# Gated cross-attention and mixture block on one core: the value matmuls with float32 values as 32-column weights in four column groups and float32 probabilities moving

## The reference, cut to what matters

```python
# x (32, 128, 128), ctx_768 (32, 77, 96); H = 16 heads of hd = 8, E = 8 experts, 2 taken
xn, xfn = layer_norm(layer_norm(x)), layer_norm(ctx)
q = (xn @ Wq + bq).reshape(B, T, H, hd)
k = (xfn @ Wk + bk).reshape(B, N, H, hd)
v = (xfn @ Wv + bv).reshape(B, N, H, hd)
w = softmax(einsum('bthd,bnhd->bhtn', q, k) / sqrt(hd))
x = x + tanh(g_xattn) * einsum('bhtn,bnhd->bthd', w, v).reshape(B, T, D)
f = layer_norm(x)
top_vals, top_idx = top_k(f @ w_router, 2)
h = square(relu(einsum('nc,ecd->ned', f, w1)))
y = einsum('ned,edc->nec', h, w2)
x = x + tanh(g_ffn) * sum(take(y, top_idx) * softmax(top_vals))
```

## Time and profile before

| | |
|---|---|
| median of 3 runs | 432.58 us |
| the profiled execution | 432.84 us |
| its span (first to last instruction) | 431.0 us |
| granted TensorE clock, mean | 0.761 |
| PE busy | 72%, 2664 matmul records |
| DVE, ACT, POOL busy | 68%, 52%, 51% |
| DMA packets | 36.57 MB, mean 85 GB/s |

### The profile page before, as it was taken

How to read it: one execution, slowest core, us unless ns; L and a number is a source line. 1 busy time by engine, 2 the same in 40 slices (tenths; PEclk the granted TensorE clock), 3 DMA queues, 4 the chain that set the end, 5 groups by cost and what they waited for, 6 DMA issues and landing times.

```text
span 431.0 us, 9014 instructions
## 1 busy us (share of the span) xinstructions
PE 309.2 (72%) x2664; PEld 261.7 (61%) x2664; DVE 291.7 (68%) x956; ACT 224.9 (52%) x490; POOL 221.8 (51%) x261
## 2 busy tenths in 40 slices
PE   0502693779399849885997869885888599699566
PEld 0301472667388738874786748774777488587455
DVE  5524744875577787868785787877887678847432
ACT  1210353556356765676565646764576467665222
POOL 8601353664566555755573458545754565665100
PEclk9965555555559975998598958995999589769869
DMA  2346019001831075206530382229211821050140
GB/s 51 100 87 93 2 44 142 5 2 42 143 125 75 33 116 157 106 28 105 159 119 8 78 170 75 75 75 159 96 75 57 146 97 78 27 198 2 47 174 24
DMA packets 29314, 36.57 MB, mean 85 GB/s; under 512 B 5849, under 2 KB 22874, under 8 KB 29274
## 3 DMA queue, kind: packets, MB, share of 16 engines
q1 hardware_dynamic: 28474, 35.05, 33.1%
q0 software_dynamic: 512, 1.06, 0.9%
q10 hardware_dynamic: 288, 0.00, 0.0%
HBM read 23.14 MB, written 2.23 MB: 59 GB/s over the span
## 4 chain that ended last, share of the span: by engine, by line
PE 39%; DVE 23%; issue 13%; DMA 11%; SPq 5%; POOL 4%; ACT 3%; DVEq 1%; POOLq 0%; ACTq 0%
PE y L533 10%; DMA qs<-q_lo 8%; PE ab L455 6%; PE s L477 5%; SPq L313 4%; DVE u L947 3%; DVE negm L831 3%; PE c L493 3%; DVE xn L782 3%; PE h L524 2%; PE ab L437 2%; DMA gb<-gates_scratch 2%; PE h L526 2%; PE h L525 2%; DVE x L867 2%
## 5 line engine op out<-in xcount | busy, mean ns | idle before, releaser
L1079 POOL TENSOR_TENSOR p_lo<-p,p_hi 77x512 f16<-77x512 f32 x128 | 147.8, 1158 | 109.9 <-ACT p L681 109.7
L831 DVE TENSOR_REDUCE negm<-ab 128x4 f32<-128x308 f32 x128 | 58.9, 470 | 72.7 <-PE ab L455 69.8
L455 PE MATMUL ab<-ks,qs 96*128 96x312 f32 x128 | 62.8, 495 | 39.8 <-DMA qs<-q_lo 27.4
L680 ACT ACTIVATE p_hi<-s 77x512 f16<-77x512 f32 x128 | 74.8, 585 | 31.2 <-PE s L477 30.9
L533 PE MATMUL y<-w2s,hs 128*128 128x128 f32 x512 | 74.2, 293 | 6.1 <-ACT hs L688 6.0
L477 PEld LDWEIGHTS s<-qs,ks 104*77 104x77 f32 x512 | 70.1, 194 | 10.9 <-issue 4.8
L681 ACT ACTIVATE p<-s 77x512 f32<-77x512 f32 x128 | 74.8, 584 | 0.0
L533 PEld LDWEIGHTS y<-w2s,hs 128*128 128x128 f32 x512 | 67.5, 206 | 8.1 <-ACT hs L688 7.4
L477 PE MATMUL s<-qs,ks 104*77 104x128 f32 x512 | 72.0, 280 | 0.2 <-ACT p L681 0.2
L455 PEld LDWEIGHTS ab<-ks,qs 96*128 96x128 f32 x128 | 31.1, 244 | 47.0 <-issue 33.9
L688 ACT ACTIVATE hs<-u 128x512 f32<-128x512 f32 x64 | 40.2, 628 | 31.3 <-DVE u L947 29.1
(11 more groups left out here) (100 smaller groups left out, 503.7 us busy)
## 6 DMA issues: line engine op xcount, KB each, us to landing
gb<-gates_scratch SPq DMA_DIRECT2D x16, 768.0 KB, 4.2
qs<-q_hi SPq DMA_DIRECT2D x16, 256.0 KB, 5.7
gb<-gates_scratch SPq DMA_DIRECT2D x8, 512.0 KB, 3.6
ks<-k_hi SPq DMA_DIRECT2D x64, 39.0 KB
x_sb<-in_x_dram SPq DMA_DIRECT2D x8, 256.0 KB, 6.7
qs<-q_lo SPq DMA_DIRECT2D x8, 256.0 KB, 6.9
x_res<-in_x_dram SPq DMA_DIRECT2D x8, 256.0 KB, 6.8
out_dram<-y_out SPq DMA_DIRECT2D x8, 256.0 KB, 5.8
```

The costliest lines, as they stand in the source:

```text
L455: nc.tensor.matmul(p[:, 0:J * NP].rearrange("t (i n) -> t i n", n=NP), qs[0:QR, par, c, T * j:T * j + T], ks[0:QR, par, c, :, NP * j:NP * ...
L680: nc.scalar.activation(p_hi[:, c, :], src, ACT.Exp).then_inc(hi_done, 1)
L831: nc.vector.tensor_reduce(negm[:, :, c], bank_ab[bank][:, 0:J * NP].rearrange("t (i n) -> t i n", n=NP)[:, :, 0:N], AX.X, ALU.max, negate= ...
L1079: nc.gpsimd.tensor_tensor(p_lo[:, c, :], p32[:, c, :], p_hi[:, c, :], ALU.subtract).then_inc(lo_done, 1)
```

## The change

The probabilities stay float32, `p` alone, and are the moving operand (128 tokens a head); the weights are the values of a head in float32: 32 columns, of which 8 are the values, one is the ones column, and the rest zeros. The four heads of a call go to four groups of 32 partitions of the bank `c`. Heads of c = 0 and 1 fill the same 128 columns of that bank, those of even c the first 16 rows of a group and those of odd c the second, and are summed there since each adds zeros to the other's rows; c = 2 and 3 fill the next 128. The result has heads down the partitions, so ACT copies it to `oT` (128x256), PE turns it in two transposes (`turn_heads`) into a shared bank (a new use `o` in each slot), and DVE divides from there. The second exponential, POOL's subtraction, the splitting of the values and the sum over the parts are gone. DVE's reading of the heads comes after the router's logits. POOL fills the value tensor with zeros and ones at the start.

```diff
-    (-1, "turn2"), (0, "s1c2"), (-1, "route2"), (0, "s1d2"), (1, "k"), (0, "mT2"), (1, "q"), (0, "s1a3"),
-    (0, "s1b3"),
...
+    (-1, "turn2"), (0, "s1c2"), (-1, "route2"), (0, "s1d2"), (-1, "o3"), (1, "k"), (0, "mT2"), (1, "q"),
+    (0, "s1a3"), (0, "s1b3"),
...
-POST = ["summed", "recip", "scaled", "x1", "stats", "moments", "normed"]
+POST = ["recip", "x1", "stats", "moments", "normed"]
...
-    VC = HD * PARTS + 1
+    VC = 2 * HD
+    VT = 2 * VC
...
-        vs = sb("vs", [N, 2, G, H, VC], BF16)
+        vs = sb("vs", [N, 2, G, H, VT])
...
-        p_hi = sb("p_hi", [N, LR, CH * T], F16)
-        p_lo = sb("p_lo", [N, LR, CH * T], F16)
+        oT = sb("oT", [CH * VT, 2 * T])
...
                 if c == 0:
-                    pe.wait_ge(split_v, at(SPLIT, s, "lo"))
+                    bank, k = ab(s, "v")
+                    pe.wait_ge(v_done, s + 1)
+                    pe.wait_ge(ab_taken[bank], k)
+                    if not loop and n == 0:
+                        pe.wait_ge(v_ones, ONES)
                     if loop or n > 0:
-                        pe.wait_ge(post_d, at(POST, n - 1, "recip"))
-                pe.wait_ge(lo_done, m + 1)
+                        pe.wait_ge(o_taken, n)
+                pe.wait_ge(p_done, m + 1)
+                r = T * (c // 2)
                 for i in range(J):
-                    h, k = NC * i + c, T * i
-                    for part in (p_hi, p_lo):
-                        mm = nc.tensor.matmul(bank_c[:, VC * h:VC * h + VC], part[:, c, k:k + T],
-                                              vs[:, par, j, h, :], start=(c == 0 and i == 0 and part is p_hi),
-                                              stop=(part is p_lo), skip_group_check=True)
+                    mm = nc.tensor.matmul(bank_c[VT * i:VT * i + VT, r:r + T], vs[:, par, j, NC * i + c, :],
+                                          p32[:, c, T * i:T * i + T], start=(c == 0), stop=(c % 2 == 1),
+                                          skip_group_check=True)
                 mm.then_inc(pv_done, 1)
+
+            def turn_heads(s, par, j, loop=False):
+                pe.wait_ge(o_taken, G * s + j + 1)
+                p, ready = claim(s, f"o{j}", loop)
+                for r in range(2):
+                    mm = nc.tensor.transpose(p[:, T * r:T * r + T], oT[:, T * r:T * r + T], ident[:, :])
+                mm.then_inc(ready, 1)
...
                         scoresT(*near[0], 1, loop)
+                    if near[-1]:
+                        turn_heads(*near[-1], loop)
...
                 bank, n = ab(s, "v")
                 if loop or s >= 2:
                     act.wait_ge(pv_done, NC * G * (s - 1))
+                else:
+                    act.wait_ge(v_ones, ONES)
                 act.wait_ge(ab_ready[bank], n)
-                nc.scalar.activation(vs[:, par, :, :, 0:HD * PARTS].rearrange("n b h (d a) -> n a (b h) d", a=PARTS)[:, 0],
-                                     bank_ab[bank][0:N, :].rearrange("n (c d) -> n c d", d=HD), ACT.Copy,
-                                     scale=col(GX, N)).then_inc(hi_v, 1)
-                if loop or s > 0:
-                    act.wait_ge(split_v, at(SPLIT, s - 1, "rest"))
-                nc.scalar.activation(v32[:, :, :].rearrange("n b d -> n (b d)"), bank_ab[bank][0:N, :], ACT.Copy,
-                                     scale=col(GX, N)).then_inc(ab_taken[bank], 1)
+                for odd, done in enumerate((v_done, ab_taken[bank])):
+                    k = VC * odd
+                    nc.scalar.activation(vs[:, par].rearrange("n b (m o) k -> n o (b m) k", o=2)[:, odd, :, k:k + HD],
+                                         bank_ab[bank][0:N, :].rearrange("n (m o d) -> n o m d", o=2, d=HD)[:, odd],
+                                         ACT.Copy, scale=col(GX, N)).then_inc(done, 1)
+
+            def evacuate_heads(s, par, j):
+                act.wait_ge(pv_done, NC * (G * s + j) + NC)
+                nc.scalar.activation(oT[:, :], bank_c[:, 0:2 * T], ACT.Copy).then_inc(o_taken, 1)
...
-                nc.scalar.activation(p_hi[:, c, :], src, ACT.Exp).then_inc(hi_done, 1)
                 nc.scalar.activation(p32[:, c, :], src, ACT.Exp).then_inc(p_done, 1)
...
+                    if near[-1]:
+                        evacuate_heads(*near[-1])
                     if near[0]:
                         exponent(*near[0], 1, loop)
...
-            def split_values(s, par, loop=False):
-                view = vs[:, par, :, :, 0:HD * PARTS].rearrange("n b h (d a) -> n a (b h) d", a=PARTS)
-                v = v32[:, :, :].rearrange("n b (h d) -> n (b h) d", d=HD)
-                rest = v_rest[:, :, :].rearrange("n b (h d) -> n (b h) d", d=HD)
-                bank, n = ab(s, "v")
-                dve.wait_ge(ab_taken[bank], n)
-                yield from split(s, "v", split_v, v, rest, [view[:, a] for a in range(PARTS)])
...
             def attended(s, par, j, loop=False):
 
                 n = G * s + j
-                dve.wait_ge(pv_done, NC * n + NC)
-                view = bank_c[:, 0:VC * H].rearrange("t (h v) -> t h v", v=VC)
-                nc.vector.tensor_reduce(o[:, :].rearrange("t (h d) -> t h d", d=HD),
-                                        view[:, :, 0:HD * PARTS].rearrange("t h (d a) -> t h d a", a=PARTS),
-                                        AX.X, ALU.add).then_inc(post_d, 1)
+                bank, k = ab(s, f"o{j}")
+                view = bank_ab[bank][:, 0:VC * H].rearrange("t (h v) -> t h v", v=VC)
+                dve.wait_ge(ab_ready[bank], k)
                 nc.vector.reciprocal(rden[:, :].rearrange("t (h o) -> t h o", o=1),
-                                     view[:, :, HD * PARTS:VC]).then_inc(post_d, 1)
+                                     view[:, :, HD:HD + 1]).then_inc(post_d, 1)
                 yield
                 dve.wait_ge(post_d, at(POST, n, "recip"))
-                nc.vector.tensor_tensor(o[:, :].rearrange("t (h d) -> t h d", d=HD),
-                                        o[:, :].rearrange("t (h d) -> t h d", d=HD),
+                nc.vector.tensor_tensor(o[:, :].rearrange("t (h d) -> t h d", d=HD), view[:, :, 0:HD],
                                         rden[:, :].rearrange("t (h o) -> t h o", o=1).broadcast_to([T, H, HD]),
-                                        ALU.mult).then_inc(post_d, 1)
+                                        ALU.mult).then_inc(ab_taken[bank], 1)
                 yield
                 if j == 0:
                     dve.wait_ge(res_in[par], landed(s, par))
                     if loop or s >= 2:
                         dve.wait_ge(y_added, s - 1)
-                dve.wait_ge(post_d, at(POST, n, "scaled"))
-                nc.vector.tensor_tensor(x1[:, par, j, :], x_res[:, par, j, :], o[:, :], ALU.add).then_inc(post_d, 1)
+                dve.wait_ge(ab_taken[bank], k)
+                nc.vector.tensor_tensor(x1[:, par, j, :].rearrange("t (i r e) -> t i r e", i=J, r=2),
+                                        x_res[:, par, j, :].rearrange("t (i r e) -> t i r e", i=J, r=2),
+                                        o[:, :].rearrange("t (r i e) -> t i r e", i=J, r=2), ALU.add).then_inc(post_d, 1)
...
-            nc.vector.memset(vs[:, :, :, :, HD * PARTS:VC], 1.0).then_inc(ones_made, 1)
...
                         finish(sf, pf, loop)
-                    take(post)
                     take(top_scores)
                     if near[-2]:
                         routed(*near[-2])
                     take(top_scores)
+                    take(post)
                     take(post)
                     if near[-2]:
                         low_x(*near[-2])
...
-            def low_part(s, par, j, c):
-
-                m = NC * (G * s + j) + c
-                pool.wait_ge(hi_done, m + 1)
-                pool.wait_ge(p_done, m + 1)
-                nc.gpsimd.tensor_tensor(p_lo[:, c, :], p32[:, c, :], p_hi[:, c, :],
-                                        ALU.subtract).then_inc(lo_done, 1)
...
             nc.gpsimd.memset(ks[:, 0, 2:4].bitcast(F32), 0.0).then_inc(zeroed[0], 1)
+            nc.gpsimd.memset(vs[:, :, :, :, :], 0.0).then_inc(v_ones, 1)
+            pool.wait_ge(v_ones, 1)
+            for odd in range(2):
+                k = VC * odd + HD
+                nc.gpsimd.memset(vs[:, :, :, :, :].rearrange("n p b (m o) k -> n o (p b m) k", o=2)[:, odd, :, k:k + 1],
+                                 1.0).then_inc(v_ones, 1)
...
-                    if near[0]:
-                        low_part(*near[0], 0)
...
```

More of the change, by code:

```diff
@@ L57 @@
 NORM_P = ["cvar_eps", "crstd", "var_eps", "rstd"]
-SPLIT = ["rest", "mid", "lo"]
 MAXP = ["hi", "lo"]
-POST = ["summed", "recip", "scaled", "x1", "stats", "moments", "normed"]
+POST = ["recip", "x1", "stats", "moments", "normed"]
 LATE = ["top", "x_lo"]
@@ L208, in flamingo_kernel @@
         s2_ready = sem("s2_ready")
[L209 to L210 removed]
+        p_done, pv_done, o_taken = sem("p_done"), sem("pv_done"), sem("o_taken")
```

(2 more changed lines are left out.)

37 lines of the change are left out of this document (7 added, 30 removed).

## The result

The changed kernel takes 461.38 us in the median of 4 runs (460.88 to 465.57), against 432.05 us (431.19 to 435.71) for the kernel before beside it. The ratio is **1.066 (95% interval 1.058 to 1.075): slower**, by 29 us. The forecast was 476, with a range of 416 to 524. The direction and the waits came as forecast; the sum was 15 us too large, and some of its terms were wrong by more than that in opposite directions.

The account below looks back on a forecast made before the run. The prediction took PE to bound the portion behind the DMA landing. Six periods +41, splitting -5, start +4, end +16 and clock -13 sum to +43 on 432.84 us: 476 us, range 416 to 524.

Parts of the forecast that it names:

- PE bounds the portion behind the landing: From the first scores after the low queries' DMA landing, PE is busy 25.5 of 28.6 us, so it sets the pace.
- the start: POOL's clearing of the new value tensor ahead of the first normalisation, with two fills of ones: +4 us.
- The calls: Value matmuls on PE: five record times of eight, +0.36 us (high clock) or +0.86 (low) a call, +7.0 a period.
- Side by side: Rival: a call's column groups overlap fully, 0.24 us (high clock) or 0.43 (low); middle 420 us; chance 0.30.
- drain: Rival: PE drains at each change of tiling, 0.19 us a change, 0.38 a call; +35, 511 us; chance 0.10.
- The heads' turn: Two PE transposes (0.4 us) plus a wait for DVE's copy of the logits (0.55 us), three times: +2.9 us a period.
- The relief: DVE loses its reduction and normalises faster, -3.0 us a period; value splitting gone, -5; ACT and POOL savings hidden behind PE.
- The clock: Between 72 and 118 us, denser PE work lifts the clock from 0.50 to 0.84: -13 us, from bounds of nothing and 13.
- The end: From 340.9 to 396 us: 27 calls +15, seven turns of the heads +7, less 6 for POOL pieces and idle PE: +16.
- the pairs of records 0.12 us apart: Sign of being right: value records start in pairs about 0.12 us apart at the high clock.
- a call of 0.25 to 0.35 us: Sign of being wrong: value calls on PE this short, instead of the 0.55 to 0.7 us expected.

Follow-up runs that it names:

- wide: The changed kernel with weights 128 columns wide in each of a call's four matmuls, mixing up the heads' results; 511.61 us.
- one_group: The changed kernel with all four heads of a call on the same 32 columns, most of their output left out; 543.81 us.
- relief: The kernel before without the second exponential and POOL's subtractions, the high float16 part of the probabilities in both value matmuls; 423.41 us, ratio 0.969.
- late: The changed kernel with the heads' two transposes behind the first expert's hidden matmuls, DVE's normalisation moved accordingly; 453.04 us, ratio 1.040.

## Why the prediction was right in direction and too high

**PE bounds the portion behind the landing: right.** The chain went to PE (57%, forecast over 50%), POOL to 16% (under 20%), the start came 3.8 us later (forecast 4).

**The calls: the term that was mis-sized.** The step was "the second must wait for the first in the same columns, while the next group's first record may run beside it. That makes 5 record times of 8". I took the two records of one head to be neighbours. They are not: the four groups' first records start within 20 ns, then the four second ones. From the first start to the last there are not four record times but one and a little (0.153 us). Against that, the sum had no term for the change of tile width, because the earlier trace rows show a narrow matmul without a gap behind it. The gaps of `wide` and `one_group` show 0.18 and 0.27 us for a switch and back. Side by side and drain, two rivals that I had given separate chances, are both true, and each alone would have been wrong: +0.22 and +0.42 us for a single call, against my +0.36 and +0.86. In six periods that is at most 6 x (6 x 0.42 + 5 x 0.22) = 22 us instead of 42, and some 20 when the two pairs of calls in a period are counted as pairs. The rule of the Trainium skill that I had left out of the sum (TensorEngine Tiling (Array Packing), Key Properties: a change of tiling mode drains TensorE) agrees with these gaps; the earlier trace rows were one transposing matmul, and I let one row, of an instruction that behaves as full width, stand for the case. Its price was below the rival's 0.19 a change, which came from a row at the low clock: 0.13 to 0.14 at that clock, 0.09 at the high one.

**The heads' turn: right.** The wait is 0.5 us, 28 times, DVE's logits as releaser. Taking two thirds of it away returned 11 us. The transposes are 0.42 to 0.66 us, against 0.4 in the sum; 18 of them are some 10 us. Together about 18 us in six periods, 17 forecast.

**The relief: too large, and by the wrong part.** In six periods I had -18 for DVE, of which 8 were its normalisation beside POOL's subtractions and 10 the reduction, and -5 for the splitting; for the work of ACT and POOL itself I had nothing there, because they are 3% and 4% of the chain. The runs show that the loss of the exponentials and subtractions is worth 13 us over the whole execution, and that of the reduction and the splitting nothing that can be measured. The failed sentence is "all of which I let count, since it ends PE's 3.1 us of idle time". DVE's largest gain is the wait for the gates, and that stands directly ahead of the wait for the DMA. An engine's small share of the chain doesn't bound what its relief brings. The 35 us of DVE's busy time that went in `relief` with no instruction less point to POOL's subtractions; no run takes away the exponentials or the subtractions alone.

**The clock: wrong.** The -13 us didn't come. The granted clock stayed at 0.50 (1.2 GHz) from 75 to 125 us with PE busy for 42 of 50 us. I had weighed "nothing" and 13 and taken the end that made the sum smaller, on a likeness of the work and no row. Nor is it shown that a higher clock would have paid 13 us: one run of the kernel before was granted 0.888 in the mean and took 431.42 us, while the 16 others beside it took 429.96 to 439.33 at 0.754 to 0.782.

**The end: too large.** +16 forecast, +4.5 measured; 27 calls at 0.3 are 8 us and the transposes some 4. `late` did not change the end either, so I take it that idle time there covers most of it.

Put together from the pieces, the six periods come to 20 + 18 - 13 = +25 us, against +24.7 in the profiled pair; that they meet so closely is chance, too. The relief is the loosest of them: in the profiled executions of `relief` and the kernel before, its six periods differ by 6.6 us only. The errors of the sum had opposite signs: the calls 22 us and the end 11 too high; the relief saves 10 us less than the -23 of DVE and the splitting, and the clock 13 less. The sum came near (+43 against +33 in the profiled pair) because they cancel, and that is luck. Of the signs that I had named, the pairs of records 0.12 us apart and a call of 0.55 to 0.7 us did not show: 0.35 us did (0.59 at the low clock), and a call of 0.25 to 0.35 us was among the signs of being wrong.

## What to carry to other kernels

- Column groups of narrow float32 weights do run side by side, but every switch to them and back costs. Before you put a narrow call between full-width matmuls, count the switches; before you pack calls together to save switches, look at what they cover where they stand.
- A wait that stands directly ahead of a DMA wait costs nothing as long as the transfer lands later anyway, however long the list of waits makes it. Add the two before pricing a relief, and add up a wait's lines under all the names that the list gives it. A move of one small piece of work off its waiting place (`late`) returned 11 us.
- Work on one engine can be paid for on another: without the exponentials and POOL's subtractions the same DVE instructions took 35 us less. A chain that shows 4% for POOL doesn't show this.
- Where a page's rule and a single row disagree, ask whether the row is the same case (here a transpose), and give the rule its term.

## What the runs showed of the hardware that I had not expected

- Float32 matmuls on four column groups: the first records of the four groups start within 20 ns, the second records 133 ns later at the high clock and 215 ns at the low one. First to last start of 8 records: 0.153 and 0.235 us, against 0.788 and 1.495 us in one group.
- A change between full-width and 32-column tiles: 0.09 us each way at the high clock, 0.13 to 0.14 at the low one. Between two narrow calls in a row there is no such gap. A transposing matmul whose weights are 32 columns wide (L454) ahead of a call counts as full width here: 0.204 us from its start to the first value record, against 0.114 in `wide`, and none of it in the earlier trace rows, where it stands among full-width ones.
- DVE's normalisation from one SBUF tensor to another stands still beside POOL's fills: 1.11 us without one, 5.14 with two, and 10.26 with two, POOL's issue of three DMAs and a third fill.
- DVE's normalisation of the heads' result takes 0.754 us in the median beside POOL's subtractions and 0.339 without them.
